# Depthwise 5x5 convolution: the third block of strips 1 to 3 in a bank of its own, its plane one column to the left

## The chip, the cores and the metric

The kernel runs on one core of one Trainium2 chip. The metric is the device time of one execution in microseconds (us). The kernel before has a median of 845.55 us over three runs (845.35 to 846.17).

## The reference

The input `x` holds 128 images of 55x55 pixels with 96 channels, in fp32. Every channel has a 5x5 filter of its own. The output is the input plus its convolution with that filter, zeros taken beyond the edges:

```python
k = jnp.transpose(kernel, (1, 2, 0))[:, :, None, :]
y = lax.conv_general_dilated(x, k, window_strides=(1, 1), padding='SAME',
                             dimension_numbers=('NHWC', 'HWIO', 'NHWC'), feature_group_count=ch)
return x + y
```

## The kernel before

The plane of 55x55 pixels is cut into 5x5 blocks of 11x11 pixels. A row of five blocks is called a strip (strips 0 to 4), and the blocks of a strip are numbered 0 to 4 from left to right (`squares` in the code). The kernel works channel by channel, 96 in all, and within a channel block by block in the order of strips and blocks.

A block is computed on TensorE. Its 121 pixels lie on the partitions, the 128 images are the columns of the loaded weights (`x_high`, `x_low`), and what is streamed past them is a window of a table `matrix`, which GpSimd builds for each channel from its filter. That table has, for each of the 121 pixels, a grid of 15 rows of 20 columns (`ROW = 20`). It is worked twice, as a high and a low part, since fp32 numbers are split in two for the fp32r matmul; so each block takes three matmuls: low input by high table (line 369), high input by low table, and high input by high table (both line 373). All three add up in one region of PSUM. An 11x11 block reaches two pixels beyond its edges, so it gives 15 rows of 15 columns, fewer at the edge of the plane: 13 columns in blocks 0 and 4, 13 rows in strips 0 and 4.

The matmul's width is made even, and starts at an even column of the plane: `even_start` and `even_end` (lines 54 to 59). So blocks 1, 2 and 3 take 16 columns from plane columns 8, 20 and 30, and blocks 0 and 4 take 14 columns from 0 and 42. Function `window` works out where this begins in a grid row of 20 columns: `left = even_start(square) - (SQUARE * square - HALO) + 1`. That is column 3 for block 0, 0 for block 1, 1 for block 2, 0 for block 3 and 1 for block 4.

PSUM has eight banks, and they are used in turn. `tiles_of_plane` (line 62) says which blocks share a bank: (0,1,2), (3,4) in strips 0 and 4, and (0,1), (2,3), (4) in strips 1 to 3, 13 banks a channel. Within a bank, a row of the plane has `pitch` columns, from the first block's first column to the last block's last, and the overlap of neighbours in a bank is summed there. A bank is used again eight banks later: `wait_bank` makes TensorE wait until it has been emptied.

ScalarE empties a bank by one copy into `y_out` (line 259), less the rows and columns that an earlier bank has already written. VectorE then adds these seams: the top four rows and the left four columns (line 313). Between, in an order written out by hand, ScalarE rounds the input of the next channel to its high part (line 249), and VectorE does the same for strip 0 (line 287) and forms the low part (line 296). SyncE's queue loads each channel's input (1600 KB, four buffers) and stores each channel's output (1520 KB, three buffers).

Of the kernel before, what the change touches and what calls it, by code (L numbers as in the profile page):

```python
# [14 lines left out]
HALO = TAPS // 2  # L15
P = 128

SQUARE = 11
ACROSS = SIDE // SQUARE
# [26 lines left out]
def start_of(k):  # L46
    return max(0, SQUARE * k - HALO)


def end_of(k):  # L50
    return min(SIDE, SQUARE * (k + 1) + HALO)


def even_start(c):
    return start_of(c) // 2 * 2


def even_end(c):
    return (end_of(c) + 1) // 2 * 2


def tiles_of_plane():
    tiles = []
    for strip in range(ACROSS):
        ends = strip in (0, ACROSS - 1)
        left = 0
        for squares in ((0, 1, 2), (3, 4)) if ends else ((0, 1), (2, 3), (4,)):
            lo, hi = start_of(squares[0]), end_of(squares[-1])
            origin = even_start(squares[0])
            tiles.append(dict(  # L70
                strip=strip, squares=squares, origin=origin, pitch=even_end(squares[-1]) - origin,
                top=start_of(strip), seam_rows=end_of(strip - 1) if strip else start_of(strip),
                bottom=end_of(strip), lo=lo, seam_cols=left if left else lo, hi=hi))
            left = hi
    return tiles


TILES = tiles_of_plane()
TILE_COUNT = len(TILES)


def adds_of(tile):
    return (tile["seam_rows"] > tile["top"]) + (tile["seam_cols"] > tile["lo"])
# [7 lines left out]
def build(nc, consts, later, x, out):  # L91
    with ExitStack() as ctx:  # L92
# [40 lines left out]
        def sums(c, t, rows, cols):  # L133

            tile = TILES[t]
            height = tile["bottom"] - tile["top"]
            plane = psum[:, bank_of(c, t), 0:height * tile["pitch"]].rearrange("p (h w) -> p h w", w=tile["pitch"])
            return plane[:, rows[0] - tile["top"]:rows[1] - tile["top"],
                         cols[0] - tile["origin"]:cols[1] - tile["origin"]]
# [5 lines left out]
        def strip_tiles(strip):  # L145
            return [t for t in range(TILE_COUNT) if TILES[t]["strip"] == strip]
# [3 lines left out]
        @block.sync  # L150
        def _(sp):
            def load_x(c):
                if c >= X_SLOTS:
                    sp.wait_ge(low_ready, len(PIECES) * (c - X_SLOTS + 1))
                sp.dma_start(x_in[c % X_SLOTS][:, :], x[c, :, :]).then_inc(x_loaded[c % X_SLOTS], 16)

            def store_y(c):
                sp.wait_ge(added, ADDS * (c + 1))
                sp.dma_start(out[c, :, :], y_out[c % Y_SLOTS][:, :]).then_inc(y_stored[c % Y_SLOTS], 16)

            sp.dma_start(first[:, :], consts[:, :]).then_inc(consts_loaded, 16)
            for piece in range(len(PIECES)):
                cols = piece_cols(piece)
                loaded = first_loaded[piece] if piece < len(PIECES) - 1 else x_loaded[0]
                sp.dma_start(x_in[0][:, cols], x[0, :, cols]).then_inc(loaded, 16)
            load_x(1)
            sp.dma_start(rest[:, :], later[:, :]).then_inc(later_loaded, 16)
            for c in range(2, X_SLOTS):
                load_x(c)
            for c in range(CHANNELS):  # L170
                if c + X_SLOTS < CHANNELS:
                    load_x(c + X_SLOTS)
                if c:
                    store_y(c - 1)
            c = CHANNELS - 1
            for a, b in LAST_STORES:
                sp.wait_ge(added, ADDS * c + ADDS_BEFORE[strip_tiles(b - 1)[-1] + 1])
                done = SIDE * start_of(a)
                end = SIDE * start_of(b) if b < ACROSS else OUT_COLS
                sp.dma_start(out[c, :, done:end], y_out[c % Y_SLOTS][:, done:end]).then_inc(y_stored[c % Y_SLOTS], 16)  # L180
            for slot in range(Y_SLOTS):
                count = len(range(slot, CHANNELS, Y_SLOTS)) + (len(LAST_STORES) - 1) * (c % Y_SLOTS == slot)
                sp.wait_ge(y_stored[slot], 16 * count)
# [152 lines left out]
        @block.tensor  # L336
        def _(pe):
            def wait_bank(c, t):

                n = c * TILE_COUNT + t - BANKS  # L340
                if n < 0:
                    return
                before, tile = n // TILE_COUNT, n % TILE_COUNT
                if adds_of(TILES[tile]):
                    pe.wait_ge(added, ADDS * before + ADDS_BEFORE[tile + 1])
                else:
                    pe.wait_ge(copied, n + 1)

            def window(c, strip, square, parts):

                top = start_of(strip) - (SQUARE * strip - HALO)
                left = even_start(square) - (SQUARE * square - HALO) + 1
                grid = matrix[c % SLOTS][0:PIXELS, parts, :].rearrange("p a (h w) -> p a h w", w=ROW)
                return grid[:, :, top:top + end_of(strip) - start_of(strip),
                            left:left + even_end(square) - even_start(square)]

            for c in range(CHANNELS):
                pe.wait_ge(matrix_step, 4 * (c + 1))
                for t, tile in enumerate(TILES):
                    strip = tile["strip"]  # L360
                    if t == strip_tiles(strip)[0] and strip in [a for a, _ in PIECES]:
                        piece = [a for a, _ in PIECES].index(strip)
                        pe.wait_ge(low_ready, len(PIECES) * c + piece + 1)
                    wait_bank(c, t)
                    for k in tile["squares"]:
                        rows, cols = (tile["top"], tile["bottom"]), (even_start(k), even_end(k))
                        target = sums(c, t, rows, cols)
                        at = (strip * ACROSS + k) * IMAGES
                        pe.matmul(target, x_low[c % SLOTS][0:PIXELS, at:at + IMAGES],  # L369
                                  window(c, strip, k, slice(HIGH, HIGH + 1)).squeeze(1),  # L370
                                  start=k == tile["squares"][0], stop=False, skip_group_check=True)
                        for part in (LOW, HIGH):
                            product = pe.matmul(target, x_high[c % SLOTS][0:PIXELS, at:at + IMAGES],  # L373
                                                window(c, strip, k, slice(part, part + 1)).squeeze(1),
                                                start=False, stop=part == HIGH and k == tile["squares"][-1],
                                                skip_group_check=True)
                    product.then_inc(sums_done, 1)
# [45 lines left out]
```

## Time and profile before

| | before |
|---|---|
| median of three runs | 845.55 us |
| the profiled execution, its own time | 845.39 us |
| its span, first to last instruction | 843.4 us |
| TensorE busy | 832.9 us, 99% |
| VectorE busy | 728.6 us, 86% |
| ScalarE busy | 617.9 us, 73% |
| GpSimd busy | 248.5 us, 29% |
| DMA moved | 309.29 MB, mean 367 GB/s |

The profiled execution's own time is 2.0 us more than its span: what lies around the first and last instruction. Matmuls overlap one another in the trace and their ends are modelled, so a matmul's own duration (about 0.28 us) says little. What a block costs is read from starts: from the start of its first matmul (line 369) to the start of the next block's.

### The profile page before, as it was taken

The numbers are of one execution on the slowest core, as the hardware profiler recorded it, in microseconds if no ns is written. First come the engines' busy times: TensorE is split into PE (matmuls) and PEld (weight loads), VectorE is DVE, ScalarE is ACT, GpSimd is POOL, SyncE is SP. The second block draws the span as 40 slices with busy tenths as digits, with TensorE's granted clock in tenths as the row PEclk, the third lists the DMA queues.
The fourth block names the chain that finished last, engine by engine and source line by source line (L and its number), as shares of the span: only waits on it lengthen the run. The fifth ranks groups of instructions, "written<-read, shape, count | busy, mean of one in ns | idle before, by whom it ended". The sixth has DMA issues, their size and how long they took to land.

```text
span 843.4 us, 20670 instructions
## 1 busy us (share of the span) xinstructions
PE 832.9 (99%) x7200; PEld 832.7 (99%) x7200; DVE 728.6 (86%) x2212; ACT 617.9 (73%) x1442; POOL 248.5 (29%) x460
## 2 busy tenths in 40 slices
PE   6999999999999999999999999999999999999998
PEld 6999999999999999999999999999999999999998
DVE  6888888888888888888888888888888888888886
ACT  5777677777767777777767777776777777776775
POOL 5223322323133231322323222223223231332310
PEclk9999999999999999999999999999999999999999
DMA  9999999999999999999999999999999999999965
GB/s 375 406 422 361 372 376 362 376 358 387 368 368 370 372 377 371 362 373 378 370 365 368 369 374 371 373 371 382 365 360 380 368 370 373 369 370 376 374 265 223
DMA packets 28615, 309.29 MB, mean 367 GB/s; under 512 B 3168, under 2 KB 3296, under 8 KB 4064
## 3 DMA queue, kind: packets, MB, share of 16 engines
q1 hardware_dynamic: 28512, 307.98, 97.3%
q8 instruction: 57, 0.93, 0.4%
q14 instruction: 46, 0.38, 0.1%
HBM read 158.55 MB, written 149.42 MB: 365 GB/s over the span
## 4 chain that ended last, share of the span: by engine, by line
PE 99%; POOL 0%; DMA 0%; issue 0%; ACT 0%; DVE 0%; DVEq 0%
PE sums L373 66%; PE sums L369 33%; DMA first<-consts 0%; POOL matrix L228 0%; POOL expanded L217 0%; POOL taps L207 0%; POOL spare L204 0%; POOL taps L201 0%; ACT y_out L259 0%; DVE y_out L313 0%; DVEq L92 0%
## 5 line engine op out<-in xcount | busy, mean ns | idle before, releaser
L373 PE MATMUL sums<-matrix,x_high 121*128 121x240 f32 (+3 forms) x4800 | 832.4, 282 | 0.0
L373 PEld LDWEIGHTS sums<-matrix,x_high 121*128 121x128 f32 x4800 | 738.1, 192 | 0.0
L369 PE MATMUL sums<-matrix,x_low 121*128 121x240 f32 (+3 forms) x2400 | 674.6, 281 | 7.0 <-POOL matrix L228 7.0
L259 ACT ACTIVATE y_out<-sums 128x99 f32<-128x99 f32 (+6 forms) x1248 | 416.6, 379 | 216.4 <-PE sums L373 196.2
L369 PEld LDWEIGHTS sums<-matrix,x_low 121*128 121x128 f32 x2400 | 461.0, 192 | 7.0 <-POOL matrix L228 7.0
L313 DVE TENSOR_TENSOR y_out<-sums,y_out 128x60 f32<-128x60 f32 (+6 forms) x1824 | 360.1, 228 | 101.5 <-ACT y_out L259 16.2
L296 DVE TENSOR_TENSOR x_low<-x_in,x_high 121x1280 fp32r<-121x1280 f32 (+1 forms) x288 | 366.3, 1272 | 5.3 <-ACT x_high L249 2.0
L228 POOL TENSOR_TENSOR matrix<-expanded,first 121x300 fp32r<-121x300 f32 x192 | 131.5, 706 | 559.9 <-PE sums L373 559.7
L249 ACT ACTIVATE x_high<-x_in 121x1280 fp32r<-121x1280 f32 x192 | 245.0, 1276 | 5.2 <-DMA x_in<-x 5.2
L217 POOL TENSOR_TENSOR expanded<-taps,first 121x100 f32<-121x100 f32 x192 | 85.3, 464 | 7.5
L287 DVE CAST x_high<-x_in 121x640 fp32r<-121x640 f32 x96 | 47.1, 490 | 4.3 <-DMA x_in<-x 3.7
L207 POOL TENSOR_TENSOR taps<-rest,spare 121x100 fp32r<-121x100 f32 x23 | 12.9, 561 | 1.8
L204 POOL TENSOR_TENSOR spare<-taps,first 121x100 f32<-121x100 f32 x24 | 9.2, 384 | 1.9
L201 POOL TENSOR_TENSOR taps<-rest,first 121x100 fp32r<-121x100 f32 x23 | 8.7, 380 | 1.9
L262 ACT ACT_TABLE_LOAD x1 | 1.3, 1283 | 0.7 <-PEq L416 0.7
L201 POOL TENSOR_TENSOR taps<-first 121x100 fp32r<-121x100 f32 x1 | 0.4, 377 | 2.2 <-DMA first<-consts 2.2
L315 DVE MEMSET warm<- 128x1 f32 x1 | 0.1, 59 | 0.8 <-PEq L416 0.8
L207 POOL TENSOR_TENSOR taps<-first,spare 121x100 fp32r<-121x100 f32 x1 | 0.4, 394 | 0.1
L262 ACT ACTIVATE warm<-warm 128x1 f32<-128x1 f32 x1 | 0.2, 203 | 0.0
L416 POOL MEMSET const-float32-0.0<- 128x1 f32 x1 | 0.1, 98 | 0.2 <-issue 0.2
L317 DVE MEMSET y_out<- 128x15 f32 x3 | 0.1, 71 | 0.0
L416 POOL MEMSET const-bfloat16-1.0<- 128x1 bf16 x1 | 0.1, 102 | 0.0
(2 smaller groups left out, 0.2 us busy)
## 6 DMA issues: line engine op xcount, KB each, us to landing
x_in<-x SPq DMA_DIRECT2D x95, 1600.0 KB, 10.6
y<-y_out SPq DMA_DIRECT2D x95, 1520.0 KB, 12.3
x_in<-x SPq DMA_DIRECT2D x2, 640.0 KB, 5.0
rest<-later SPq DMA_DIRECT2D x1, 1150.0 KB, 11.4
y<-y_out SPq DMA_DIRECT2D x1, 852.5 KB, 3.5
y<-y_out SPq DMA_DIRECT2D x1, 365.0 KB, 2.3
x_in<-x SPq DMA_DIRECT2D x1, 320.0 KB, 3.0
y<-y_out SPq DMA_DIRECT2D x1, 302.5 KB, 2.6
```

The costliest lines, as they stand in the source:

```text
L201: pool.tensor_tensor(by_channel(taps[0:PIXELS, HIGH, :]), by_channel(source), identity, ALU.add).then_inc(taps_step, 1)
L204: pool.tensor_tensor(by_channel(spare[0:PIXELS, :]), by_channel(taps[0:PIXELS, HIGH, :].bitcast(F32)), identity, ALU.subtract).then_inc(ta ...
L207: pool.tensor_tensor(taps[0:PIXELS, LOW, :], source, spare[0:PIXELS, :], ALU.subtract).then_inc(taps_step, 1)
L217: pool.tensor_tensor(expanded[0:PIXELS, part, :].rearrange("p (d a e) -> p d a e", d=TAPS, e=TAPS), rows.unsqueeze(2).broadcast_to([PIXELS ...
L228: pool.tensor_tensor(matrix[c % SLOTS][0:PIXELS, part, :].rearrange("p (b d q) -> p b d q", d=TAPS, q=ROW), expanded[0:PIXELS, part, :].re ...
L249: act.activation(x_high[c % SLOTS][0:PIXELS, cols], x_in[c % X_SLOTS][0:PIXELS, cols], ACT.Copy).then_inc(high_ready, 1)
L259: act.activation(outputs(c, rows, cols), sums(c, t, rows, cols), ACT.Copy).then_inc(copied, 1)
L287: dve.tensor_copy(x_high[c % SLOTS][0:PIXELS, cols], x_in[c % X_SLOTS][0:PIXELS, cols]).then_inc(cast_done, 1)
L296: dve.tensor_tensor(x_low[c % SLOTS][0:PIXELS, cols], x_in[c % X_SLOTS][0:PIXELS, cols], x_high[c % SLOTS][0:PIXELS, cols].bitcast(F32), A ...
L313: dve.tensor_tensor(y, sums(c, t, rows, cols), y, ALU.add).then_inc(added, 1)
L369: pe.matmul(target, x_low[c % SLOTS][0:PIXELS, at:at + IMAGES], window(c, strip, k, slice(HIGH, HIGH + 1)).squeeze(1), start=k == tile["sq ...
L373: product = pe.matmul(target, x_high[c % SLOTS][0:PIXELS, at:at + IMAGES], window(c, strip, k, slice(part, part + 1)).squeeze(1), start=Fa ...
```

## The change

In strips 1 to 3 the banks hold blocks (0,1), (2), (3,4). There block 2 starts at plane column 19 and ends at 35, where it ran from 20 to 36: its width stays at 16 columns, and its window begins at column 0 of the grid row, where it began at 1. All else is as it was: the order of the blocks, three matmuls for each, 13 banks a channel, strips 0 and 4.

```diff
-def even_start(c):
-    return start_of(c) // 2 * 2
+def left_of(strip, square):
+    alone = square == 2 and 0 < strip < ACROSS - 1
+    return start_of(square) - 1 if alone else start_of(square) // 2 * 2
 
-def even_end(c):
-    return (end_of(c) + 1) // 2 * 2
+def right_of(strip, square):
+    width = end_of(square) - left_of(strip, square)
+    return left_of(strip, square) + (width + 1) // 2 * 2
...
-        for squares in ((0, 1, 2), (3, 4)) if ends else ((0, 1), (2, 3), (4,)):
+        for squares in ((0, 1, 2), (3, 4)) if ends else ((0, 1), (2,), (3, 4)):
             lo, hi = start_of(squares[0]), end_of(squares[-1])
-            origin = even_start(squares[0])
+            origin = left_of(strip, squares[0])
             tiles.append(dict(
-                strip=strip, squares=squares, origin=origin, pitch=even_end(squares[-1]) - origin,
+                strip=strip, squares=squares, origin=origin, pitch=right_of(strip, squares[-1]) - origin,
...
-                left = even_start(square) - (SQUARE * square - HALO) + 1
+                left = left_of(strip, square) - (SQUARE * square - HALO) + 1
...
-                            left:left + even_end(square) - even_start(square)]
+                            left:left + right_of(strip, square) - left_of(strip, square)]
...
-                        rows, cols = (tile["top"], tile["bottom"]), (even_start(k), even_end(k))
+                        rows, cols = (tile["top"], tile["bottom"]), (left_of(strip, k), right_of(strip, k))
```

TensorE in strip 1, blocks 0 to 4, before. Each block has two rows, its first matmul and the two with the high input; the shape is that of the region written in PSUM (partitions x rows x columns, or one run of columns where a bank's rows follow one another without a gap), and a wait for `added` is that for the bank:

```order
L369 MATMUL sums<-matrix,x_low 128x15x14 [waits added,low_ready]
L373 MATMUL sums<-matrix,x_high 128x15x14 x2
L369 MATMUL sums<-matrix,x_low 128x15x16
L373 MATMUL sums<-matrix,x_high 128x15x16 x2
L369 MATMUL sums<-matrix,x_low 128x15x16 [waits added]
L373 MATMUL sums<-matrix,x_high 128x15x16 x2
L369 MATMUL sums<-matrix,x_low 128x15x16
L373 MATMUL sums<-matrix,x_high 128x15x16 x2
L369 MATMUL sums<-matrix,x_low 128x210 [waits added]
L373 MATMUL sums<-matrix,x_high 128x210 x2
```

And now (two lines were added above, so 369 and 373 are 371 and 375):

```order
L371 MATMUL sums<-matrix,x_low 128x15x14 [waits added,low_ready]
L375 MATMUL sums<-matrix,x_high 128x15x14 x2
L371 MATMUL sums<-matrix,x_low 128x15x16
L375 MATMUL sums<-matrix,x_high 128x15x16 x2
L371 MATMUL sums<-matrix,x_low 128x240 [waits added]
L375 MATMUL sums<-matrix,x_high 128x240 x2
L371 MATMUL sums<-matrix,x_low 128x15x16 [waits added]
L375 MATMUL sums<-matrix,x_high 128x15x16 x2
L371 MATMUL sums<-matrix,x_low 128x15x14
L375 MATMUL sums<-matrix,x_high 128x15x14 x2
```

The third wait for a bank stands ahead of block 3, where it stood ahead of block 4. Block 2 now fills a bank's rows without a gap, and block 4 no longer does.

VectorE in strip 1, the seams of its three banks (top rows, then left columns), before and now:

```order
L313 TENSOR_TENSOR y_out<-sums,y_out 128x4x24 [waits added,copied]
L313 TENSOR_TENSOR y_out<-sums,y_out 128x4x22 [waits added,copied]
L313 TENSOR_TENSOR y_out<-sums,y_out 128x15x4
L313 TENSOR_TENSOR y_out<-sums,y_out 128x4x9 [waits added,copied]
L313 TENSOR_TENSOR y_out<-sums,y_out 128x15x4
```

```order
L315 TENSOR_TENSOR y_out<-sums,y_out 128x4x24 [waits added,copied]
L315 TENSOR_TENSOR y_out<-sums,y_out 128x4x11 [waits added,copied]
L315 TENSOR_TENSOR y_out<-sums,y_out 128x15x4
L315 TENSOR_TENSOR y_out<-sums,y_out 128x4x20 [waits added,copied]
L315 TENSOR_TENSOR y_out<-sums,y_out 128x15x4
```

Eleven columns of the top seam have moved from the second bank to the third. ScalarE's copies follow suit: 11x22 and 11x9 elements before, 11x11 and 11x20 now.

## Rows read from the trace of the kernel before

**Rows 1.** The page, busy time: us (share of the span) and instructions.
```profile
PE 832.9 (99%) x7200; PEld 832.7 (99%) x7200; DVE 728.6 (86%) x2212; ACT 617.9 (73%) x1442; POOL 248.5 (29%) x460
```

**Rows 2.** The chain that ended last, share of the span by engine.
```profile
PE 99%; POOL 0%; DMA 0%; issue 0%; ACT 0%; DVE 0%; DVEq 0%
```

**Rows 3.** TensorE's only wait: us in total, times, longest.
```profile
PE sums L369 <- POOL matrix L228: 7.0, 1, 7.0
```

**Rows 4.** Timeline of TensorE, one channel's strip 2: start, duration, line, tile, count.
```profile
402.01 0.28 PE L369 MATMUL sums<-matrix,x_low 121*128 121x210 f32 x1
...
402.34 0.28 PE L369 MATMUL sums<-matrix,x_low 121*128 121x240 f32 x1
...
402.69 0.29 PE L369 MATMUL sums<-matrix,x_low 121*128 121x240 f32 x1
402.81 0.44 PE L373 MATMUL sums<-matrix,x_high 121*128 121x240 f32 x2
403.08 0.28 PE L369 MATMUL sums<-matrix,x_low 121*128 121x240 f32 x1
403.20 0.39 PE L373 MATMUL sums<-matrix,x_high 121*128 121x240 f32 x2
403.43 0.28 PE L369 MATMUL sums<-matrix,x_low 121*128 121x210 f32 x1
...
403.77 0.28 PE L369 MATMUL sums<-matrix,x_low 121*128 121x210 f32 x1
```

**Rows 5.** The same view: blocks 2 and 3 of strip 1, fourth and last channel.
```profile
37.63 0.29 PE L369 MATMUL sums<-matrix,x_low 121*128 121x240 f32 x1
...
38.02 0.28 PE L369 MATMUL sums<-matrix,x_low 121*128 121x240 f32 x1
...
833.43 0.29 PE L369 MATMUL sums<-matrix,x_low 121*128 121x240 f32 x1
...
833.82 0.28 PE L369 MATMUL sums<-matrix,x_low 121*128 121x240 f32 x1
```

**Rows 6.** The same view: strip 4 from its block 1 on, next channel's start.
```profile
405.85 0.28 PE L369 MATMUL sums<-matrix,x_low 121*128 121x208 f32 x1
...
406.19 0.29 PE L369 MATMUL sums<-matrix,x_low 121*128 121x208 f32 x1
...
406.54 0.27 PE L369 MATMUL sums<-matrix,x_low 121*128 121x208 f32 x1
...
406.87 0.27 PE L369 MATMUL sums<-matrix,x_low 121*128 121x182 f32 x1
...
407.20 0.28 PE L369 MATMUL sums<-matrix,x_low 121*128 121x182 f32 x1
```

**Rows 7.** Groups by shape: count | busy us, mean ns | idle before, releaser.
```profile
L259 ACT ACTIVATE y_out<-sums 128x242 f32<-128x242 f32 x288 | 112.0, 389 | 33.7 <-PE sums L373 33.7
...
L259 ACT ACTIVATE y_out<-sums 128x99 f32<-128x99 f32 x288 | 79.1, 275 | 0.0
...
L313 DVE TENSOR_TENSOR y_out<-sums,y_out 128x88 f32<-128x88 f32 x288 | 72.0, 250 | 31.1 <-ACT y_out L259 1.4
L313 DVE TENSOR_TENSOR y_out<-sums,y_out 128x36 f32<-128x36 f32 x288 | 56.6, 196 | 31.2 <-DVE y_out L313 1.4 <-ACT y_out L259 0.2
...
L313 DVE TENSOR_TENSOR y_out<-sums,y_out 128x80 f32<-128x80 f32 x96 | 23.3, 242 | 10.2 <-ACT y_out L259 0.2
```

**Rows 8.** Timeline of VectorE: the seams of strip 1, of strip 2, of strip 3 on.
```profile
402.31 1.17 DVE L313 TENSOR_TENSOR y_out<-sums,y_out 128x96 f32<-128x96 f32 x5
...
404.80 1.16 DVE L313 TENSOR_TENSOR y_out<-sums,y_out 128x96 f32<-128x96 f32 x5
...
407.27 1.57 DVE L313 TENSOR_TENSOR y_out<-sums,y_out 128x96 f32<-128x96 f32 x6
```

**Rows 9.** Two stretches: us, busy (count) by engine, clock, DMA share, GB/s.
```profile
40.00:60.00 20.00, 20.00 (x176) 20.00 (x175) 17.40 (x53) 15.04 (x37) 4.21 (x8) 1.00 1.01 425
...
300.00:400.00 100.00, 100.00 (x870) 100.00 (x869) 87.63 (x266) 73.22 (x175) 29.68 (x55) 1.00 1.00 370
```

**Rows 10.** The page: all that the DMA moved.
```profile
DMA packets 28615, 309.29 MB, mean 367 GB/s; under 512 B 3168, under 2 KB 3296, under 8 KB 4064
```

## The prediction

> **What bounds the kernel now.** I read the busy times first, then the chain of work that ended last, then the waits. TensorE is busy for 832.9 of 843.4 us [rows 1], it makes up 99% of the chain [rows 2], and it waits once, for 7.0 us at the start, until the first table is built [rows 3]. No later wait stands against it. So the end is set by how fast one block's matmuls follow the other's, and each microsecond taken from a block that repeats comes off the total, as long as no other engine turns up behind.
>
> What each block costs is read from the timeline of TensorE, from the start of its first matmul to the start of the next block's. In strip 2 of one channel [rows 4] the starts of blocks 0 to 4 and of the next strip are 402.01, 402.34, 402.69, 403.08, 403.43 and 403.77. So the five blocks take 0.33, 0.35, 0.39, 0.35 and 0.34 us. Block 2 stands out by 0.04 us against blocks 1 and 3, which have the same 240 columns; the pair of its high products is recorded with 0.44 us, that of block 3 with 0.39 [rows 4].
>
> The view rounds to 10 ns, so I took means over the starts of blocks 1 to 4 in strips 1 to 3 of the 93 channels from the fourth on, 279 strips; the first and the last of block 2 in strip 1 are shown, 37.63 to 38.02 and 833.43 to 833.82 [rows 5]. Block 1 takes 345 ns, block 2 takes 393 and block 3 takes 349. The spread of block 2 over all these is 0.39 to 0.40: it is not a wait that comes now and then but a cost that every one pays.
>
> What sets block 2 apart? Its window is the only one that is 16 columns wide and starts at column 1 of a grid row. Blocks 1 and 3 are as wide and start at 0. Block 4 starts at 1 and block 0 at 3, but both are 14 wide and take no more than 0.34 us. Strip 4 says the same on 13 rows instead of 15 [rows 6]: blocks 1, 2 and 3, each 208 columns, take 0.34, 0.35 and 0.33 us, and block 2, again from column 1, is the longest. The excess is smaller there, since something else already sets about 0.33 us: 182, 208 and 210 columns all take about that [rows 4, 6].
>
> **The change part by part.**
>
> Block 2 reads from column 0. By the reading above it then costs what blocks 1 and 3 cost, (345 + 349) / 2 = 347 ns in place of 393: 46 ns less. There are 3 such blocks in 96 channels, 288, so 288 x 0.046 = 13.2 us. All of it lies on the path that sets the end. The bounds come from the nearest rows: block 2 might fall to the 0.335 us of blocks 0 and 4 in the mean of the same 279 strips (58 ns less, 16.7 us), or only to block 3's 349 (44 ns less, 12.7 us). I take the middle of blocks 1 and 3, since they have the same shape and start.
>
> The banks are opened by other blocks: 0, 2 and 3, where they were 0, 2 and 4. The number of waits, three a strip, stays. Block 3 opens one now. Strip 4's block 3 opens a bank already, and it is the shortest of its three at 0.33 us [rows 6]. So I cost it at nothing; the price if this is wrong is a rival below.
>
> The copies and seams keep their number and their sum. ScalarE's copies of 242 and 99 elements take 389 and 275 ns, so 0.8 ns an element [rows 7]. The new ones, of 121 and 220, come to about 293 and 371 by that line (an estimate from these two rows): 664 as before. VectorE's top seams of 88 and 36 take 250 and 196 [rows 7]. The new ones have 44, about 204 by the line between these two, and 80, measured at 242: 446 as before.
>
> What does shift is the end of a strip: the third bank's copy is about 0.1 us longer and its seam about 0.05. Behind these wait VectorE's next seams, and TensorE for the bank eight banks on. The cover is wide. The seams of strip 2 start at 404.80 and are over by 405.96 [rows 8]; its banks are next wanted from the following channel's first block on, at 407.20 [rows 6], which leaves 1.2 us by the end of the whole group. The seams of strip 1 start at 402.31 and end by 403.48 [rows 8]; the first of their banks is wanted by what is now strip 3's block 3, three blocks after 403.77 [rows 4], about 404.8: 1.3 us. The group that begins with strip 3's seams ends by 408.84 [rows 8], and the first of these banks is used again by block 2 of the next channel's strip 1. A strip takes 403.77 - 402.01 = 1.76 us [rows 4] and a channel (833.43 - 37.63) / 92 = 8.65 us [rows 5], so this block starts at 402.69 - 1.76 + 8.65 = 409.58: 0.7 us. The 0.15 us and the faster pace of TensorE leave this above zero. VectorE's busy share goes from 86% to 88% [rows 1], since its work is unchanged in a shorter time.
>
> Sum against the profiled execution's own time: 845.39 - 13.2 = 832.2 us. That execution lies 0.16 us below the median of the runs, which is nothing here.
>
> **The rivals.**
>
> The transfers become the bound. The trace moves 309.29 MB [rows 10]; in 832.2 us less the 2 us around the span this needs 373 GB/s, against 367 now. For this rival speaks that the DMA share is 1.00 in the steady stretch at 370 GB/s [rows 9]. Against it speaks the stretch from 40 to 60 us, which moves 425 GB/s [rows 9], so 370 is no ceiling. And TensorE waits for nothing after the start [rows 3], so no load or store is late for it now. If 370 GB/s were the ceiling, the time would be 309.29 MB / 370 GB/s = 836 us of span, 838 in all. The Trainium skill, "DMA: Bandwidth & Descriptors", section Specifications, names about 358 GB/s as the HBM limit of a core and 368 as the vendor's derate. By 368 the span would be at least 840.5 us and the gain under 3 us; by 358 even the time before would not have been possible, so the trace speaks against both.
>
> Opening a bank is what costs, not where the window starts. Before, block 2 of strips 1 to 3 is the only block of 240 columns that opens a bank. Then block 2 stays at 393 ns, and block 3, which now opens a bank too, rises by the same 46 ns: 288 x 0.046 = 13.2 us more, 858.6 us. This is the case on the other side. It decides as soon as an opening 240-column block costs more than a following one. Against it: strip 4's block 3 opens a bank at 208 columns and is the shortest of its width [rows 6], and block 2 there does not open one and is the longest.
>
> Block 4 loses its gapless bank. It has its window at column 1 like block 2, and could be spared only because its 14 columns are written as one run of 210. If it paid block 2's excess of 46 ns once it is written with a pitch of 26, the gain of block 2 would be eaten: 845.4 us, no change. Against it: strip 4's block 4 already shares a bank with that pitch and takes 0.33 us [rows 6], and block 0 with a pitch of 24 takes 0.33 us against block 4's 0.34 [rows 4]. The Trainium skill, "Advanced Engine Details and Errata", section PSUM Cachelines, says that any non-contiguous access pattern slows matmuls significantly. By that rule block 2 would gain and block 4 lose, as in this rival; the rows of block 0 and block 4 differ by no more than 0.01 us in the wrong direction, so the trace does not bear it out at this width.
>
> The change doesn't reach the cost: block 2's excess has a cause that stays, such as its place in the strip. Also 845.4 us.
>
> **How the numbers follow.** Forecast, block 2 at the cost of its neighbours: 0.87, at 832.2 us. Transfers or another engine take back most of the gain, 836 to 841 us: 0.04. No change by either of the last two rivals: 0.05. Opening a bank costs: 0.04. Faster by over 0.2% is the first two, 0.91; within 0.2%, which is about what a measurement of this kernel can tell from no change, 0.05; slower 0.04. The range covers the forecast with the bounds of block 2's new cost, 845.4 - 16.7 = 828.7 and 845.4 - 12.7 = 832.7; I widen the upper end to 834.5, since the single channel shown gives 0.04 us a block at 10 ns rounding, 11.5 us in all, and half a microsecond lies between runs. The other cases, 0.13, stay outside.
>
> **What would show each step.** In the timeline after, block 2 of strips 1 to 3 should take 0.34 to 0.35 us, blocks 0, 1, 3 and 4 what they took, strips 0 and 4 the same, and a channel 8.51 us in place of 8.65. TensorE should still wait only at the start, and copies and seams should show the new shapes at the old sums. The prediction is wrong if block 2 stays at 0.39, if block 3 or 4 of these strips grows, or if TensorE waits for `added`, for the table or for a load. If block 2 falls and the time does not, the stretches will show a DMA rate stuck near 370 GB/s.

## The result: slower, 859.5 us where 832.2 were forecast

The changed kernel takes 859.47 us (median; 859.30 to 859.85) beside 845.86 for the kernel before: a ratio of 1.0161, with a 95% interval from 1.0144 to 1.0179. The sign was wrong. The time is close to the 858.6 us of the rival in which opening a bank costs, so that rival had to be tested first; it fell.

The page of the changed kernel, the lines that answer to [rows 1 to 3]:

```profile
span 857.4 us, 20670 instructions
...
PE 843.5 (98%) x7200; PEld 826.4 (96%) x7200; DVE 748.9 (87%) x2212; ACT 624.1 (73%) x1442; POOL 348.0 (41%) x460
...
PE 97%; issue 1%; POOL 0%; DVE 0%; ACT 0%; DMA 0%; DVEq 0%
```

VectorE's busy time rose by 20 us and GpSimd's by 100, though both execute as many instructions as before, on as many elements in sum. The waits of the same kernel (us in total, times, longest):

```profile
PEld sums L371 <- DVE y_out L315: 14.4, 65, 0.3
PE sums L371 <- POOL matrix L230: 7.1, 1, 7.1
...
DVE y_out L315 <- ACT y_out L261: 3.1, 7, 0.5
```

TensorE's weight loads now wait for VectorE's seams in 65 places, which they never did. The groups that grew, by shape, in the changed kernel (count | busy us, mean ns | idle before):

```profile
L298 DVE TENSOR_TENSOR x_low<-x_in,x_high 121x1280 fp32r<-121x1280 f32 x192 | 306.3, 1596 | 1.7 <-ACT x_high L251 1.6
...
L230 POOL TENSOR_TENSOR matrix<-expanded,first 121x300 fp32r<-121x300 f32 x192 | 238.1, 1261 | 474.2 <-PE sums L375 474.0
```

and the same two in the kernel before:

```profile
L296 DVE TENSOR_TENSOR x_low<-x_in,x_high 121x1280 fp32r<-121x1280 f32 x192 | 285.0, 1484 | 2.0 <-ACT x_high L249 2.0
...
L228 POOL TENSOR_TENSOR matrix<-expanded,first 121x300 fp32r<-121x300 f32 x192 | 131.5, 706 | 559.9 <-PE sums L373 559.7
```

The low part takes 112 ns longer in the mean, and building the table almost twice as long. They run side by side. The timelines of VectorE and of GpSimd in one late channel show it; GpSimd starts 0.20 us ahead, and both are slow, the low part with 1.84 us:

```profile
401.76 1.84 DVE L298 TENSOR_TENSOR x_low<-x_in,x_high 121x1280 fp32r<-121x1280 f32 x1
```
```profile
401.56 2.60 POOL L230 TENSOR_TENSOR matrix<-expanded,first 121x300 fp32r<-121x300 f32 x2 [5.42 <-PE sums L375]
```

In the kernel before the two missed each other by 0.16 us: the last low part of a channel ended at 405.87 + 1.48 = 407.35, and the table was begun at 407.51, beside the seams of [rows 8]:

```profile
405.87 1.48 DVE L296 TENSOR_TENSOR x_low<-x_in,x_high 121x1280 fp32r<-121x1280 f32 x1
```
```profile
407.51 1.35 POOL L228 TENSOR_TENSOR matrix<-expanded,first 121x300 fp32r<-121x300 f32 x2 [6.47 <-PE sums L373]
```

TensorE in the same channel, first matmul of each block, strip 1 from block 1 on, and strip 2:

```profile
403.29 0.28 PE L371 MATMUL sums<-matrix,x_low 121*128 121x240 f32 x1
...
403.82 0.38 PE L371 MATMUL sums<-matrix,x_low 121*128 121x240 f32 x1
...
404.27 0.37 PE L371 MATMUL sums<-matrix,x_low 121*128 121x240 f32 x1
...
404.70 0.27 PE L371 MATMUL sums<-matrix,x_low 121*128 121x210 f32 x1
...
405.37 0.28 PE L371 MATMUL sums<-matrix,x_low 121*128 121x240 f32 x1
...
405.71 0.27 PE L371 MATMUL sums<-matrix,x_low 121*128 121x240 f32 x1
...
406.05 0.28 PE L371 MATMUL sums<-matrix,x_low 121*128 121x240 f32 x1
...
406.38 0.27 PE L371 MATMUL sums<-matrix,x_low 121*128 121x210 f32 x1
```

In strip 2, where [rows 4] showed 0.35, 0.39 and 0.35, blocks 1 to 3 now take 0.34, 0.34 and 0.33 us: the change does to block 2 what was forecast, and more. In strip 1 the same blocks take 0.53, 0.45 and 0.43: there TensorE waits for a bank twice, ahead of block 2 and ahead of block 3. Such a wait is mostly hidden in the page, since the chain still reads 97% TensorE and the waiting matmul is only recorded as longer, 0.38 for 0.28. It is the distance of starts that shows it.

The two regimes also follow each other in time. By the starts of the first matmul of each channel, channels 1 to 16 (counted from 0) take 8.45 to 8.46 us, against 8.65 before [rows 5]; from there on they take 8.64 to 9.14 but for one, 8.85 in the mean of channels 20 to 89. Two stretches of the changed kernel (us, busy by engine PE, PEld, DVE, ACT, POOL, clock, DMA share, GB/s) set them side by side:

```profile
80.00:150.00 70.00, 70.00 (x623) 70.00 (x622) 61.79 (x190) 53.43 (x125) 28.97 (x40) 1.00 1.00 377
...
200.00:400.00 200.00, 199.48 (x1696) 194.49 (x1696) 177.35 (x524) 147.64 (x342) 83.33 (x109) 1.00 1.00 364
```

For these 16 channels the change was a gain of 0.2 us each. Then the kernel fell into a second regime, in which it loses 0.2.

### The profile page after: what moved, and what is told of

The parts are those of the page before. It is cut to its first block, busy times and chain, and to the rows that moved or that the text cites. A ratio compares the mean times of both kernels' runs of the same rounds, so it can differ in the third digit from the quotient of the medians.

```text
span 857.4 us, 20670 instructions
## 1 busy us (share of the span) xinstructions
PE 843.5 (98%) x7200; PEld 826.4 (96%) x7200; DVE 748.9 (87%) x2212; ACT 624.1 (73%) x1442; POOL 348.0 (41%) x460
## 4 chain that ended last, share of the span: by engine, by line
PE 97%; issue 1%; POOL 0%; DVE 0%; ACT 0%; DMA 0%; DVEq 0%
PE sums L375 63%; PE sums L371 35%; DVE y_out L315 0%; DMA first<-consts 0%; POOL matrix L230 0%; ACT x_high L251 0%; POOL expanded L219 0%; ACT y_out L261 0%; POOL taps L209 0%; POOL spare L206 0%; POOL taps L203 0%; DVEq L310 0%; DVEq L94 0%; DVE x_low L298 0%
## 5 line engine op out<-in xcount | busy, mean ns | idle before, releaser
L375 PE MATMUL sums<-matrix,x_high 121*128 121x240 f32 (+3 forms) x4800 | 822.5, 278 | 0.0
L375 PEld LDWEIGHTS sums<-matrix,x_high 121*128 121x128 f32 x4800 | 730.0, 192 | 0.0
L371 PE MATMUL sums<-matrix,x_low 121*128 121x240 f32 (+3 forms) x2400 | 682.3, 284 | 9.1 <-POOL matrix L230 7.1
L261 ACT ACTIVATE y_out<-sums 128x220 f32<-128x220 f32 (+6 forms) x1248 | 421.0, 373 | 223.4 <-PE sums L375 208.2
L315 DVE TENSOR_TENSOR y_out<-sums,y_out 128x60 f32<-128x60 f32 (+5 forms) x1824 | 359.2, 228 | 94.1 <-ACT y_out L261 3.1
L230 POOL TENSOR_TENSOR matrix<-expanded,first 121x300 fp32r<-121x300 f32 x192 | 238.1, 1261 | 474.2 <-PE sums L375 474.0
L298 DVE TENSOR_TENSOR x_low<-x_in,x_high 121x1280 fp32r<-121x1280 f32 (+1 forms) x288 | 387.3, 1345 | 5.0 <-ACT x_high L251 1.6
L219 POOL TENSOR_TENSOR expanded<-taps,first 121x100 f32<-121x100 f32 x192 | 80.5, 440 | 7.5
L209 POOL TENSOR_TENSOR taps<-rest,spare 121x100 fp32r<-121x100 f32 x23 | 10.4, 453 | 1.8
```

The lines of the kernel that those rows point to most:

```text
L209: pool.tensor_tensor(taps[0:PIXELS, LOW, :], source, spare[0:PIXELS, :], ALU.subtract).then_inc(taps_step, 1)
L219: pool.tensor_tensor(expanded[0:PIXELS, part, :].rearrange("p (d a e) -> p d a e", d=TAPS, e=TAPS), rows.unsqueeze(2).broadcast_to([PIXELS ...
L230: pool.tensor_tensor(matrix[c % SLOTS][0:PIXELS, part, :].rearrange("p (b d q) -> p b d q", d=TAPS, q=ROW), expanded[0:PIXELS, part, :].re ...
L261: act.activation(outputs(c, rows, cols), sums(c, t, rows, cols), ACT.Copy).then_inc(copied, 1)
L298: dve.tensor_tensor(x_low[c % SLOTS][0:PIXELS, cols], x_in[c % X_SLOTS][0:PIXELS, cols], x_high[c % SLOTS][0:PIXELS, cols].bitcast(F32), A ...
L315: dve.tensor_tensor(y, sums(c, t, rows, cols), y, ALU.add).then_inc(added, 1)
```

## The experiments

**The theory (A)** after the two traces: VectorE's queue was already all but full. Its instructions with the gaps between them need about 8.49 us a channel. This can be read in the changed kernel's first regime, where VectorE waits for nothing from one strip-1 low part to the next:

```profile
100.25 1.48 DVE L298 TENSOR_TENSOR x_low<-x_in,x_high 121x1280 fp32r<-121x1280 f32 x1
...
102.73 1.48 DVE L298 TENSOR_TENSOR x_low<-x_in,x_high 121x1280 fp32r<-121x1280 f32 x1
...
108.74 1.48 DVE L298 TENSOR_TENSOR x_low<-x_in,x_high 121x1280 fp32r<-121x1280 f32 x1
```

108.74 - 100.25 = 8.49 us, and 8.57 in every fourth channel. TensorE with the cheap block 2 needs 8.45, so VectorE falls a little behind in each channel. GpSimd's table is triggered by TensorE. So it creeps ahead against VectorE's work: in channel 7 it starts 0.66 us after the last low part, in channel 16 only 0.21 us after it, which is 0.05 us a channel. In the stretch above it already starts inside the last low part, at 103.18 against 102.73, and pays for it alone:

```profile
103.18 2.25 POOL L230 TENSOR_TENSOR matrix<-expanded,first 121x300 fp32r<-121x300 f32 x2 [3.31 <-PE sums L375]
```

In channel 17 it starts first, by 0.11 us, and that is the first channel that takes longer. Later it is mostly 0.2 us ahead, and the low part takes 0.36 us longer: 8.49 + 0.36 = 8.85, the second regime. **The rivals**: opening a bank with a 240-column block costs (B), or VectorE has the 13% of slack that its busy share suggests and something else holds the seams.

**Only the banks.** The changed kernel with block 2 back at plane column 20:

```diff
-    return start_of(square) - 1 if alone else start_of(square) // 2 * 2
+    return start_of(square) // 2 * 2
```

> The changed kernel with block 2 of strips 1 to 3 back at plane column 20 (window at column 1): only the banks are re-divided. Theory A (VectorE's queue is the bound behind TensorE, and the change passes it): block 2 stays near 393 ns, a channel at 8.65 us, time 845 to 846 us, since TensorE is no faster. Theory B (opening a bank with 240 columns costs): blocks 2 and 3 both near 393 ns, about 858 us. If writing without a gap is what made block 2 cheap, block 2 falls to about 337 ns and the time is near the changed kernel's 859 us.

Measured: 846.12 us beside 846.02, ratio 1.0001 (0.9992 to 1.0010). The timeline of TensorE, strip 1, blocks 1 to 4:

```profile
401.40 0.28 PE L371 MATMUL sums<-matrix,x_low 121*128 121x240 f32 x1
...
401.75 0.29 PE L371 MATMUL sums<-matrix,x_low 121*128 121x240 f32 x1
...
402.14 0.28 PE L371 MATMUL sums<-matrix,x_low 121*128 121x240 f32 x1
...
402.48 0.28 PE L371 MATMUL sums<-matrix,x_low 121*128 121x210 f32 x1
```

0.35, 0.39, 0.34: block 3 opens a bank at no price, and block 2, alone in its bank and written without a gap, is as dear as ever: 394, 393 and 394 ns in strips 1 to 3, the means of 92 channels from the fourth on by the trace's unrounded starts, and the same three numbers in the kernel before. Rival B is out. Neither bank, nor gap, nor place makes block 2 dear, and the new division of copies and seams costs nothing.

**The table after the low part.** The changed kernel, with one wait more on GpSimd, for the last low part of the channel before the table's own:

```diff
                     pool.wait_ge(sums_done, TILE_COUNT * (c - SLOTS + 1))
+                    pool.wait_ge(low_ready, len(PIECES) * c)
                 for part in (HIGH, LOW):
```

> The changed kernel, with one more wait on GpSimd: the table of channel c is built only when VectorE has formed the last low part of channel c-1's successor, so that the two no longer run side by side. Theory A: the table's instructions fall from 1261 to about 700 ns and the low parts from 1596 to 1480, a channel takes what VectorE's queue needs, 8.49 us as in the first 17 channels of the changed kernel, and the time is 845.4 - 0.16 x 95 = about 830 us. Theory B and any theory in which VectorE has the 13% of slack that its busy share suggests and the loss comes from the banks: 859 us, no change from the changed kernel.

Measured: 840.14 us, ratio to the kernel before 0.993 (0.9915 to 0.9945). One added wait makes the changed kernel 19 us quicker. The groups:

```profile
L299 DVE TENSOR_TENSOR x_low<-x_in,x_high 121x1280 fp32r<-121x1280 f32 x192 | 285.0, 1485 | 1.1 <-ACT x_high L252 1.1
...
L231 POOL TENSOR_TENSOR matrix<-expanded,first 121x300 fp32r<-121x300 f32 x192 | 132.8, 712 | 555.2 <-DVE x_low L299 536.3 <-PE sums L376 18.8
```

Both are back at their old durations, so the overlap was what had slowed them. The time is 10 us above what I expected. The later channels take 8.48 to 8.87 us, 8.59 in the mean. In one of every four GpSimd also splits the filters of the next group, from 406.79 on in the channel shown, and beside that VectorE's rounding and its small low part take 0.61 and 0.90 us, where they take 0.51 and 0.82 else:

```profile
407.38 0.61 DVE L290 CAST x_high<-x_in 121x640 fp32r<-121x640 f32 x1
408.02 0.90 DVE L299 TENSOR_TENSOR x_low<-x_in,x_high 121x640 fp32r<-121x640 f32 x1
```

VectorE still sets the pace here, with a period above 8.49. From one strip-1 low part to the next it mostly takes 8.51 to 8.53 us in three channels of four, as the rounding takes 0.51 us, where it took 0.48 in the changed kernel's first channels, and 8.68 to 8.70 in the fourth, which makes 8.56. The rest of the mean comes from about one channel in nine that takes 0.1 to 0.4 us longer, with pauses of VectorE that the trace puts down to no single cause.

**VectorE lighter.** The changed kernel, with the rounding of strip 0's input on ScalarE:

```diff
-                               ACT.Copy).then_inc(high_ready, 1)
+                               ACT.Copy).then_inc(high_ready if piece else cast_done, 1)
...
+                    split_high(c + 1, 0)
                     split_high(c + 1, 1)
...
-                    cast_high(c + 1)
```

> The changed kernel, with the rounding of strip 0's input (0.49 us a channel) on ScalarE in place of VectorE. Theory A: VectorE's queue then needs about 8.0 us a channel, or 8.35 beside the table, less than TensorE's 8.46, so TensorE waits for no bank and the time is 845.4 - 0.19 x 95 = about 827 us. Theory B: still near 859 us.

Measured: 827.98 us, ratio 0.9788 (0.9772 to 0.9805), the quickest version here together with the next but one. The page and the waits:

```profile
PE 813.9 (99%) x7200; PEld 813.8 (99%) x7200; DVE 684.0 (83%) x2116; ACT 653.1 (79%) x1538; POOL 299.3 (36%) x460
```
```profile
DVE y_out L317 <- ACT y_out L261: 37.1, 94, 0.7
...
PE sums L371 <- POOL matrix L230: 6.9, 1, 6.9
```

TensorE waits only at the start again, every later channel takes 8.45 to 8.46 us, and VectorE, which now waits for 37.1 us, has room. The table still runs partly beside other work of VectorE (977 ns in the mean), which no longer matters.

**The control**, the same edit on the kernel before:

> The kernel before (block 2 at column 1, old banks), with the rounding of strip 0's input on ScalarE in place of VectorE: the control of the run that did this to the changed kernel. Theory A: TensorE sets the pace here, so a lighter VectorE is worth nothing, 845 to 846 us. If the lighter VectorE alone were what brought 828 us: below 840.

Measured: 846.48 us, ratio 1.0008 (0.9998 to 1.0017). A lighter VectorE alone is worth nothing, and so the 18 us are block 2's, set free.

**Both remedies together**, the rounding on ScalarE and the table after the low part:

> The changed kernel with both the rounding of strip 0's input on ScalarE and the table built after VectorE's last low part. Theory A: TensorE is already unhindered with the rounding moved, so the second edit brings nothing more, 827 to 829 us, but the table's instructions fall to about 710 ns. If the overlap with the table still costs something with the rounding moved: below 827 us.

Measured: 827.75 us, ratio 0.9787 (0.9771 to 0.9803), with the table's instructions at 713 ns: nothing more to be had, TensorE is unhindered.

**VectorE heavier.** The kernel before, with a memset of 400 elements more on VectorE in each channel:

```diff
+        extra = sbuf("extra", [P, 400], F32)
...
                 add_seams(c, 4)
+                dve.wait_ge(pads_zeroed, Y_SLOTS + c)
+                dve.memset(extra[:, :], 0.0).then_inc(pads_zeroed, 1)
```

> The kernel before, with one memset of 400 elements more on VectorE in each channel, about 0.45 us. Theory A (VectorE has some 0.16 us a channel to spare, not the 1.1 us of its idle share): at least 0.3 us a channel longer, 874 us or more, with TensorE waiting for the seams. Theory that VectorE's idle 14% is slack: 845.5 us.

Measured: 871.92 us, ratio 1.0305 (1.0284 to 1.0326). It is 2 us short of the least that I expected, but a little more work on an engine that is 86% busy cost 26 us. The waits:

```profile
PEld sums L372 <- DVE y_out L314: 15.8, 69, 0.8
...
DVE y_out L314 <- ACT y_out L260: 2.5, 7, 0.5
```

The pattern is that of the changed kernel, and so is its course: channels 1 to 14 take 8.64 to 8.66 us, the later ones 8.96 in the mean, once the table has come to lie beside the low part (1270 ns for its instructions). TensorE's matmuls are untouched here. A full VectorE is enough. The memset itself, recorded with 0.39 us, lengthens VectorE's period by only about 0.16, as this stretch of the first channels shows, in which VectorE waits for nothing:

```profile
76.53 1.48 DVE L297 TENSOR_TENSOR x_low<-x_in,x_high 121x1280 fp32r<-121x1280 f32 x1
...
85.18 1.48 DVE L297 TENSOR_TENSOR x_low<-x_in,x_high 121x1280 fp32r<-121x1280 f32 x1
```

85.18 - 76.53 = 8.65 us, where it was 8.49: just TensorE's pace. So the memset only fills VectorE; most of the 26 us is the last low part, which in the later channels mostly takes 1.69 to 1.79 us beside the table, in place of 1.48.

**The table put beside the low part by an added wait**, in the kernel before. GpSimd waits until all but the last two seams of strip 1 are added, and then starts just ahead of a low part:

```diff
                     pool.wait_ge(sums_done, TILE_COUNT * (c - SLOTS + 1))
+                    pool.wait_ge(added, ADDS * (c - 1) + ADDS_BEFORE[4])
                 for part in (HIGH, LOW):
```

> The kernel before, TensorE's work untouched; GpSimd builds the table later, once all but the last two seams of strip 1 are added, so that it starts a little ahead of VectorE's low part of strips 1 and 2 and runs beside it. Theory A: the low part of that stretch grows by about 0.36 us (to 1.84), VectorE's chain by as much, to some 8.85 us a channel, and the time goes to about 845.4 + 0.2 x 95 = 864 us although no matmul changed; the table's instructions take about 1300 ns. If overlap with GpSimd costs VectorE nothing, or VectorE has 1.1 us to spare: 845.5 us.

and once more with `ADDS_BEFORE[5]`, after the last of these seams, so that VectorE starts first:

> As the run with the table first, but GpSimd waits for the last seam of strip 1 too, which also releases nothing on VectorE: VectorE goes straight on to the low part, so it starts first and the table second. If the order decides who is slowed, as the first channels of the changed kernel suggest (table second: 2.25 us for two, low part still 1.48): the table's instructions take over 1100 ns, the low part stays at 1480, and the time stays at 845 to 848 us. If both suffer whatever the order: about 864 us.

Measured: table first 879.25 us, ratio 1.0405 (1.0387 to 1.0424); table second 846.21 us, ratio 1.0003 (0.9994 to 1.0013). The timelines of VectorE and GpSimd, with the table first:

```profile
401.49 1.87 DVE L297 TENSOR_TENSOR x_low<-x_in,x_high 121x1280 fp32r<-121x1280 f32 x1
```
```profile
401.32 2.60 POOL L229 TENSOR_TENSOR matrix<-expanded,first 121x300 fp32r<-121x300 f32 x2 [2.81 <-PE sums L374]
```

and with it second:

```profile
404.57 1.48 DVE L297 TENSOR_TENSOR x_low<-x_in,x_high 121x1280 fp32r<-121x1280 f32 x1
```
```profile
404.83 2.43 POOL L229 TENSOR_TENSOR matrix<-expanded,first 121x300 fp32r<-121x300 f32 x2 [4.25 <-PE sums L374]
```

The order decides. Table first, by 0.17 us: the low part takes 1.87 us. Table second, by 0.26: it keeps its 1.48, and the table pays; only its end still reaches into the next low part, which takes 1.56. The first run came out 15 us above what I expected. There TensorE waits for the table:

```profile
PEld sums L370 <- POOL matrix L229: 32.9, 83, 6.9
```

The table, in turn, waits for VectorE: from the tenth channel on it mostly starts 0.17 us after the seam that it was made to wait for, and TensorE's channel 0.05 us after the table's end. VectorE itself waits for others in only 10 of the 876.9 us. So its queue sets the pace, and the late table is where TensorE meets it. A channel in which only one low part is slowed takes 8.87 or 8.88 us, the 8.85 that I expected. In 41 channels the next low part is slowed too, to between 1.72 and 1.74 us, as GpSimd's next step then also starts ahead of it, and a channel takes about 9.13. That is what I had left out. In the second run the longer work of both fits beside the rest.

**What makes block 2 dear.** The kernel before, with the table's grid shifted by one column, so that blocks 0 to 4 read from columns 4, 1, 2, 1, 2:

```diff
-                left = even_start(square) - (SQUARE * square - HALO) + 1
+                left = even_start(square) - (SQUARE * square - HALO) + 2
...
-    b = (TAPS - 1 - (step - 1 - j) % TAPS)[:, None, :]
+    b = (TAPS - 1 - (step - 2 - j) % TAPS)[:, None, :]
...
-    q, p = np.arange(ROW).reshape(1, -1) - 1, np.arange(REACH).reshape(1, -1)
+    q, p = np.arange(ROW).reshape(1, -1) - 2, np.arange(REACH).reshape(1, -1)
```

> The kernel before, with the table's grid shifted by one column: blocks 0 to 4 now read from columns 4, 1, 2, 1 and 2 where they read from 3, 0, 1, 0 and 1; nothing else is changed. If an odd first column is what makes 16 columns dear, blocks 1 and 3 of strips 1 to 3 rise from 346 to about 393 ns and block 2 falls to about 340, so a channel is longer by 6 x 47 - 3 x 53 = 123 ns and more in strips 0 and 4, some 858 us. If every first column that is not a multiple of four is dear, block 2 stays at 393 too: 872 us or more. If it is block 2's place and not its window, nothing moves: 845.5 us.

Measured: 891.55 us, ratio 1.0544 (1.0527 to 1.0560). TensorE, strip 1, blocks 0 to 4:

```profile
403.78 0.29 PE L369 MATMUL sums<-matrix,x_low 121*128 121x210 f32 x1
...
404.14 0.30 PE L369 MATMUL sums<-matrix,x_low 121*128 121x240 f32 x1
...
404.54 0.31 PE L369 MATMUL sums<-matrix,x_low 121*128 121x240 f32 x1
...
404.95 0.30 PE L369 MATMUL sums<-matrix,x_low 121*128 121x240 f32 x1
...
405.35 0.29 PE L369 MATMUL sums<-matrix,x_low 121*128 121x210 f32 x1
```

Blocks 1, 2 and 3 all take 0.40 to 0.41 us. Not only an odd first column is dear: block 2 at the even column 2 costs 410 ns. The second run on this widens block 0 to 16 columns, from column 3:

```diff
 def even_end(c):
-    return (end_of(c) + 1) // 2 * 2
+    return 16 if c == 0 else (end_of(c) + 1) // 2 * 2
```

> The kernel before, with block 0 of every strip 16 columns wide in place of 14 (its window columns 3 to 18, the last three of the new region being zeros of the table). If 16 columns are dear from every first column that is not a multiple of four, block 0 of strips 1 to 3 rises from 335 to about 393 to 410 ns, some 0.2 us a channel with strips 0 and 4, and the time to 862 us or more. If 16 columns from column 3 cost what 16 columns from column 0 do (345 ns): about 848 us.

Measured: 868.10 us, ratio 1.0264 (1.0243 to 1.0284). TensorE, strip 2, blocks 0 and 1, that is from the start of the first to that of the second:

```profile
404.36 0.30 PE L369 MATMUL sums<-matrix,x_low 121*128 121x240 f32 x1
404.76 0.28 PE L369 MATMUL sums<-matrix,x_low 121*128 121x240 f32 x1
```

0.40 us where block 0 took 0.33 [rows 4]: 16 columns are dear from columns 1, 2 and 3, and cheap from 0. From column 4 they were not run, so that multiples of four are cheap is not shown beyond 0.

## Why the prediction was wrong

**What bounds the kernel now** was right for the kernel before: TensorE, with the rounding on ScalarE worth nothing there (1.0008).

**Block 2 reads from column 0** was right, and under-sized. With TensorE unhindered, a channel takes 8.45 us where it took 8.65: 0.20 us, or 19 us in 95 channels, against the 0.138 and 13.2 of the sum. Means of 91 channels in the run with the rounding on ScalarE give block 2 as 334 to 338 ns, not 347, and block 3 behind it as 341, not 349. So three blocks give 0.17 us, and their followers another 0.02. The nearest price was the lower bound that I named, 335 ns, though by unrounded starts that is block 4's alone (334); block 0 took 343 in the mean. So even with the cover intact the time, 827.98 us in that run, would have come out 0.7 us under the range.

**The banks are opened by other blocks, at nothing** was right (1.0001).

**The copies and seams keep their sum** was right: 121 and 220 elements on ScalarE took 280 and 368 ns, and 44 and 80 on VectorE 204 and 242.

**The step that failed is the cover.** I took the 1.2 and 0.7 us between the last seam and the next use of a bank for a reserve, and VectorE's 86% of the span [rows 1] for an engine with 14% to spare. The lead was even larger than the 0.7 us that I read to the end of a group of seams: the bank of block 2 is freed by the first seam of that group, at 407.27 + 0.25 = 407.52 [rows 8], 2.1 us ahead of its next use at 409.58. But a lead is a stock, not a rate: it is used up when VectorE needs more time a channel than TensorE. It needed about 0.05 us more, and in 17 channels the table had come ahead of the low part. From then on TensorE waited for just this bank and the next one, ahead of blocks 2 and 3 of strip 1. And the idle time was not free time. VectorE was idle for 843.4 - 728.6 = 114.8 us before, yet waited for others in only a few of them. These are all its waits in the kernel before that exceed a microsecond:

```profile
DVE y_out L313 <- ACT y_out L259: 16.2, 72, 0.6
DVE x_high L287 <- DMA x_in<-x: 3.7, 2, 3.2
DVE x_low L296 <- ACT x_high L249: 2.0, 2, 1.5
DVE y_out L313 <- DVE y_out L313: 1.9, 6, 0.5
```

16.2 us over 96 channels is 0.17 us a channel. That was the whole slack (8.65 - 0.17 = 8.48, next to the 8.49 of VectorE's period above), and the change takes 0.20. The other idle time, some 90 us over 2212 instructions, is about 40 ns between one instruction and the next, which no speed-up of TensorE gives back. The hint stood in [rows 7]: of the 31.2 us idle ahead of the 36-element seams only 1.6 had a releaser.

**The rivals** lacked the one that came. "Another engine" stood there as a way to lose part of the gain, at 836 to 841 us. An engine at its limit by itself does just that: 840 us, the run with the table held back. What turned the gain into a loss is the second step, which I did not look for: when two engines' work slides against each other, pieces that never met begin to overlap. In the trace of the kernel before this was in sight, since the table is released by TensorE's last block of a channel and lay 0.16 us behind the low part.

The Trainium skill, "SBUF — State Buffer", section Who interferes with whom, states it: a VectorE instruction with two inputs in SBUF reads its second through an interface that it shares with GpSimd, and the order of issue decides who blocks. The traces agree with both halves, 1.87 us with the table first and 1.48 with it second. They agree also in that the seams, which have one input in PSUM, ran beside the table with its instructions at 706 ns.

**The transfers** as a rival are out too: the quickest version moves the same 309 MB in a span of 825.4 us, 375 GB/s, and TensorE waits for none of it.

Open remains what makes a window of 16 columns dear from columns 1, 2 and 3, and why one of 14 columns isn't: in strips 2 and 3 block 0 took 338 ns from column 3 and 333 from column 4.

## What to carry to other kernels

Before speeding up the engine that bounds a kernel, count the time that the next engine truly waits for others, a period at a time; busy share overstates its room by all the gaps between its instructions. If the speed-up exceeds that room, the next engine sets the pace, and work of third engines that is triggered by the first slides into it; look at what lies just ahead of it in the timeline and whether the two get in each other's way. And read the first and the last periods apart: a loss that sets in after 17 of 96 channels is a drift, not a price of the change.

## What the runs showed of the hardware

A matmul that streams rows of 16 numbers of 4 bytes, 20 apart, costs more from some first columns: in the means of strips 2 and 3, three matmuls of 240 columns took 392 to 410 ns from columns 1, 2 and 3, against 337 to 350 from column 0. With 14 numbers a row the start made little difference, 330 to 342 ns from columns 1 to 4 in the same strips. The Trainium skill, "Advanced Engine Details and Errata", section SBUF Cachelines, names lines of 16 bytes and a penalty where fewer than two accesses fall on one line. If a grid row starts on a line, which no run here shows, sixteen numbers from column 0 fill four lines and from columns 1, 2 and 3 touch five, which agrees in the count of lines. It does not agree in the accesses: from column 2 every line gets at least two, and that start cost the most, 410 ns; and 14 from column 3 touch five lines, two of them once, and are not dear. The rule of the Trainium skill, "Advanced Engine Details and Errata", section PSUM Cachelines, that any gap slows matmuls significantly finds no support here: block 2 written without a gap and written with one cost the same 394, 393 and 394 ns.

GpSimd and VectorE make each other wait when the one builds a product of two SBUF tensors while the other subtracts two. In 76 low parts of the changed kernel the table had started first, by 0.11 to 0.56 us. The low part took 1.94 us where the table was 0.11 us ahead, 1.83 at 0.22, 1.66 at 0.38 and the usual 1.48 at 0.56, and in all 76 it ended 2.04 or 2.05 us after the table's start. So by these numbers it isn't slowed down as it runs: it waits until 0.56 us into the first of the table's two instructions (recorded with 0.70), and then takes its 1.48. The second of the two ended 0.55 to 0.56 us after the low part in all 76, so it waits in its turn, and the two take 2.6 us in place of 1.35. Where the low part started first, in 17 more, it kept its 1.48 us (1.51 once), and the table took up to 2.6.
